# Second convolution of a graph network: the residual addition moved from VectorE to an identity product in TensorE and a copy by ScalarE

## The reference, cut to what matters

```python
h = x @ W;  dis = rsqrt(deg)
agg = segment_sum(h[src] * (dis[src] * dis[dst])[:, None], dst) + h * (dis * dis)[:, None]
return agg + b
# around both steps:
x = _layernorm(x + gcn_layer(relu(gcn_layer(x, W1, b1)), W2, b2), axis=-1)
```

## Time and profile before

| what | value |
|---|---|
| median of 3 runs | 10529.21 us (10516.9 to 10536.39) |
| the profiled execution | 10513.06 us |
| its span, first to last instruction | 10510.6 us |
| DVE busy over the span | 8002.5 us (76%) |
| POOL busy over the span | 7840.4 us (75%) |
| PE busy over the span | 6426.3 us (61%) |
| ACT busy over the span | 5904.7 us (56%) |

### The profile page before, as it was taken

How to read it: one execution, slowest core, us unless ns; L and a number is a source line. 1 busy time by engine, 2 the same in 40 slices (tenths; PEclk the granted TensorE clock), 3 DMA queues, 4 the chain that set the end, 5 groups by cost and what they waited for, 6 DMA issues and landing times. The chain is left out here.

```text
span 10510.6 us, 142293 instructions
## 1 busy us (share of the span) xinstructions
PE 6426.3 (61%) x32436; PEld 5258.3 (50%) x32436; DVE 8002.5 (76%) x33105; ACT 5904.7 (56%) x13869; POOL 7840.4 (75%) x7586
## 2 busy tenths in 40 slices
PE   6037666667774666667755666786457675654444
PEld 3026655555664666667755666674235443432222
DVE  8359899956667999999988888655558777874444
ACT  0026577767776999978957777432125443432222
POOL 7767688867776888766637777687777777878887
PEclk8569988878886555578868888665558765765555
DMA  3999888832223777634424555464336443432222
GB/s 114 330 299 314 286 289 289 289 123 75 76 74 121 234 236 235 207 126 139 142 87 160 173 175 177 145 172 120 92 104 183 143 116 99 139 111 65 63 65 60
DMA packets 1019500, 1694.47 MB, mean 161 GB/s; under 512 B 304877, under 2 KB 535080, under 8 KB 1018594
## 3 DMA queue, kind: packets, MB, share of 16 engines
q1 hardware_dynamic: 782752, 1361.06, 38.8%
q0 software_dynamic: 175936, 218.82, 9.3%
q10 hardware_dynamic: 59970, 105.49, 2.9%
HBM read 988.03 MB, written 707.78 MB: 161 GB/s over the span
## 5 line engine op out<-in xcount | busy, mean ns | idle before, releaser
L1351 POOL DMA_INDIRECT g_got<-scaled,row_src x2352 | 2230.1, 948 | 751.5 <-issue 631.8
L903 DVE SCALAR_TENSOR_TENSOR g_sums<-g_got,first,g_sums 128x128 f32<-128x128 f32 (+3 forms) x3136 | 871.6, 278 | 1159.5 <-DMA g_got<-scaled,row_src 1148.4
L299 PE MATMUL g_a_p_z<-sb_L_gnn_W,g_a_u_t 128*128 128x128 f32 (+3 forms) x2574 | 603.8, 373 | 592.5 <-DVE g_sums L1073 197.4
L1186 ACT COPY g_a_u_t<-g_a_p_t 128x512 f32<-128x512 f32 (+3 forms) x495 | 224.8, 454 | 1222.2 <-PE g_a_p_t L1138 637.3
L907 DVE SCALAR_TENSOR_TENSOR g_sums<-g_sums,cont,g_got 128x128 f32<-128x128 f32 (+3 forms) x3128 | 881.3, 282 | 0.0
L299 PEld LDWEIGHTS g_a_p_z<-sb_L_gnn_W,g_a_u_t 128*128 128x128 f32 (+1 forms) x2574 | 443.1, 245 | 759.9 <-ACT g_a_u_t L1186 398.3
L299 PE MATMUL g_bb_p_z<-sb_L_gnn_W,g_bb_u_t 128*128 128x128 f32 (+2 forms) x4302 | 755.8, 336 | 84.7 <-DVE g_bb_z L1078 77.0
L299 PEld LDWEIGHTS g_bb_p_z<-sb_L_gnn_W,g_bb_u_t 128*128 128x128 f32 x4302 | 676.0, 237 | 135.6 <-issue 108.9
L1186 ACT COPY g_bb_u_t<-g_bb_p_t 128x1024 f32<-128x1024 f32 (+2 forms) x294 | 233.6, 795 | 774.6 <-PE g_bb_p_t L290 774.1
L2475 POOL DMA_INDIRECT gb_got<-x,row_src x392 | 404.8, 1033 | 242.1 <-POOLq L178 138.1
L458 POOL DMA_INDIRECT f_got<-in_x,idx_dst x396 | 463.2, 1170 | 139.8 <-issue 120.1
(11 more groups left out here) (496 smaller groups left out, 23955.6 us busy)
## 6 DMA issues: line engine op xcount, KB each, us to landing
raw<-gb_u SPq DMA_DIRECT2D x98, 768.0 KB, 3.9
xs<-f_o ACTq DMA_DIRECT2D x97, 516.0 KB
f_x<-in_x ACTq DMA_DIRECT2D x97, 512.0 KB
g_bb_own<-in_x SPq DMA_DIRECT2D x97, 512.0 KB
wide<-g_bb_o SPq DMA_DIRECT2D x97, 512.0 KB
g_bb_own<-wide SPq DMA_DIRECT2D x97, 512.0 KB
g_bb_res<-in_x SPq DMA_DIRECT2D x97, 512.0 KB
x<-g_bb_o SPq DMA_DIRECT2D x97, 512.0 KB
```

The costliest lines, as they stand in the source:

```text
L299: last = nc.tensor.matmul(dst_psum[0:p, q * g * width:(q * g + n) * width], turned_tile[0:n * k, q * P:q * P + p], weight[0:n * k, 0:n * w ...
L903: nc.vector.scalar_tensor_tensor(out=self.firsts, in0=new, scalar=first[:, col], in1=self.firsts, op0=ALU.mult, op1=ALU.add).then_inc(run_ ...
L1186: last = nc.scalar.copy(to, source)
L1351: pool.indirect_dma_start(got[b.s4][:, c * row:(c + 1) * row], None, table, bass.IndirectOffsetOnAxis(ap=index[:, b.n * CH + c:b.n * CH + ...
```

## The change

It holds for the `b` node of this pass alone (`joins`: it has a residual, no last weight and no edges). The product's stage on PE now also waits for `gained`, and behind each of the 8 products by the weight it adds a product of the identity matrix with the residual's 128 columns onto the same place of the bank. DVE's `rows` of b is gone from its list. A new ACT stage `take_rows` (lag 1) waits for `multiplied` and copies the bank's 1024 columns to `g_bb_z`, raising `rows_ready`; it stands between `evacuate` of a and `normalise` of a.

```diff
+                self.joins = self.normal and not self.deep and edges is None
...
-                times_weight(self.p_z, self.u_t[b.s], self.weight, p, j, self.k, self.m).then_inc(m.multiplied, 1)
+                if self.joins:
+                    nc.tensor.wait_ge(m.gained, b.n + 1)
+                    for q in range(j):
+                        to = self.p_z[0:p, q * D:(q + 1) * D]
+                        nc.tensor.matmul(to, self.u_t[b.s][:, q * P:q * P + p], self.weight[:, :], start=True, stop=False)
+                        last = nc.tensor.matmul(to, ident[0:p, 0:p], self.res_s[b.s][0:p, q * D:(q + 1) * D], start=False,
+                                                stop=True)
+                    last.then_inc(m.multiplied, 1)
+                else:
+                    times_weight(self.p_z, self.u_t[b.s], self.weight, p, j, self.k, self.m).then_inc(m.multiplied, 1)
+
+            def take_rows(self, b):
+
+                p, j = self.r.pj(b)
+                m = self.m_
+                nc.scalar.wait_ge(m.multiplied, b.n + 1)
+                if b.after(len(self.z_s)):
+                    nc.scalar.wait_ge(m.finished, b.n + 1 - len(self.z_s))
+                nc.scalar.copy(self.z_s[b.n % len(self.z_s)][0:p, 0:j * D], self.p_z[0:p, 0:j * D]).then_inc(m.rows_ready, 1)
...
-                    return self.on(lag, every, (self.factors, 3), (self.rows, 1), (self.variance, 1))
+                    return self.on(lag, every, (self.factors, 3), (self.variance, 1))
...
-                    return self.on(lag, every, (self.root, 2), (self.evacuate, 0)), self.on(lag, every, (self.normalise, 3))
+                    return (self.on(lag, every, (self.root, 2), (self.evacuate, 0)),
+                            self.on(lag, every, (self.take_rows, 1), (self.normalise, 3)))
...
-                            factors, rows, variance = others_of
-                            stages += [*in_a((na.combine, 0), (na.factors, 3)), factors, *in_a((na.rows, 1)), rows,
+                            factors, variance = others_of
+                            stages += [*in_a((na.combine, 0), (na.factors, 3)), factors, *in_a((na.rows, 1)),
...
-                            stages = in_a((na.root, 2)) + ahead + in_a((na.evacuate, 0), (na.normalise, 3)) + behind
+                            stages = in_a((na.root, 2)) + ahead + in_a((na.evacuate, 0)) + behind[:1] + in_a((na.normalise, 3)) + behind[1:]
```

## The result

The changed kernel takes 10897.12 us in the median of 4 runs (10892.56 to 10933.97), the kernel before 10525.06 (4 runs, 10516.9 to 10536.39): 1.036 times as long, 95% interval 1.0336 to 1.0385. The prediction was 10887 us, in a range of 10700 to 11060. The execution that was profiled is the longest of the four: 10933.97 us, span 10932.2.

A forecast was written before the change was run, and what follows sets the result against it. DVE was taken to bound the pass at 9.10 us a turn; the new loop's terms sum to 25.91 us for two turns, 3.85 more a turn over 93 turns, 358 us, giving 10887 us, range 10700 to 11060.

The forecast's parts named there:

- The step that decides: Wait for `gained` moves from DVE's addition to PE's product, where PE must stand still until 6.4 us later.
- The loop's way through SP's store: Normalisation, SP's store, residual load, POOL's bias, PE's product, ACT's copy, normalisation two blocks on: 25.91 us for two turns.
- The terms: Times of the steps from normalisation through store, load, bias, product, transposes, evacuations and copy, summed to 25.91 us.
- 93 x 3.85 = 358 us: Loss over the pass: 12.95 us a turn against 9.10, counted for 93 of 98 turns.
- Unequal pairs of stores: Expected in the changed profile: stores of `b` blocks 12 to 14 us apart on average, perhaps in unequal pairs.
- Taken from DVE: DVE's addition, 1.13 us of its sequence a turn; at best 0.67 won, and worth nothing behind the loop.
- POOL's floor: POOL's own work of 8.43 us a turn, limiting any gain to 0.67 us a turn, 65 us over 97 turns.
- The residual is never late for PE: Rival: PE's wait lengthens no loop and the pass falls to POOL's 8.43 us a turn, 10464 us; chance 0.07.
- Only the bank tile counts: Rival: PE and ACT on the one `g_bb_p_z` set the turn, 9.02 to 9.9 us, around 10550 us; chance 0.10.
- PE stays at the half clock: Rival: all 32 records and the transposes at half clock add 1.9 us a turn, 11064 us; chance 0.08.
- DVE's 62%: DVE's busy share in the pass, forecast to fall from 98% to about 62%.
- POOL's 65%: POOL's busy share in the pass, forecast to fall to about 65%.

The follow-up runs named there:

- e2: Kernel before, with PE's product of a `b` block also waiting for the biased residual it does not read, no work added: 10798 us, 1.0257 of before.
- e3: Changed kernel without PE's wait for `gained`; the identity multiplies the bias row, and POOL's bias frees the residual buffer: 10491 us, 0.9967 of before.
- e1: Changed kernel with the residual loads of `a` and `b` blocks one turn earlier, into four buffers instead of two: 10493 us, 0.9965 of before.
- e7: Changed kernel with the `b` residual first, not last, among a turn's loads in SP's list: 10857 us, 1.0316 of the kernel before.
- e11: Changed kernel run once more, unedited, for a second trace: 10902 us (one run), 12.73 us a turn.
- e5: The kernel of e1 with the transposes of `b` ahead of its product in PE's list: 10740 us, 1.0208 of the kernel before.
- e9: Changed kernel with the identity product in two pieces of 512 columns instead of eight of 128, opening each bank: 10906 us, 1.0355 of before.

## Why the prediction was right

The place of the loss, its mechanism and its size came out as argued.

*The step that decides*, the wait for `gained` moved to PE, is shown by e2 (wait alone: slower by 266 us), e3 (all the work, no wait: faster) and e1 (wait kept, residual earlier: faster). The loop's way through SP's store is shown by e1 and, in sign, by e7; that the buffers were not what held the loads back is read from SP's waits, since e1 changed both at once.

*The terms* as measured in the loop above, against the predicted: store to load 3.03 (2.87 + 0.03); issue to bias 7.25 (7.03); bias to product 2.49 (2.35); product 6.28 (5.35); transposes to evacuation 1.08 (1.05); evacuations 0.91 and 0.47 (1.01 and 0.48); copy 0.91 (1.01); normalisations 1.55 and 3.20 (1.56 and 3.17). The sum is 27.17 against 25.91, three quarters of the difference being the product: I had put half of its 32 records at the low pace, and in the timeline 24 of them ran at it (0.63 us a pair, the last six records 0.39 a pair), at a granted clock of 0.56 in the mean. The alternating pattern's ring goes through such a slow product too, since its other product, which does not wait, lies beside the ring. What shortens it is above all the landing. Followed ring by ring through the timelines (45 rings of e11, 61 of the even part of the first profile), it took 6.5 us from issue to bias in the mean against 7.4, and the product 5.9 against 6.1; two turns took 25.9 against 27.2 us. Why the load lands sooner there stays open.

*The turns.* 93 x 3.85 = 358 us were predicted for the pass; store to store the first profile has 397 more than before, e11 359 (1235.0 against 875.9). The median of the runs lies 5 us from e11's execution. Part of the closeness (10 us) is luck. In e11's mean the product was half a microsecond longer than the 5.35 I had taken, and the landing half a microsecond shorter than the 7.03, so that two errors cancel in the sum of 25.91; in the even pattern of the first profile both were longer than predicted. Unequal pairs of stores had been named as possible, but not that they would be the shorter pattern; and PE, which was to wait in nearly every turn, does so in the first profile (80 times) but only in every second turn of e11.

*Taken from DVE:* worth nothing behind the loop, as predicted, and worth 39 us (10531.9 to 10492.7) once the loop is opened, of at most 65 that POOL's floor allowed.

*The rivals.* "The residual is never late for PE" would have given 10464; that is what e1 brought about, at 10493. "Only the bank tile counts" is excluded by e1: with the bank tile's loop unchanged the turn falls to POOL's 8.47. "PE stays at the half clock" was half true: of e11's products two that had waited ran at 0.55 (above) and 0.71, and one that had not at 1.00.

```profile
1825.88:1830.92 5.04, 5.04 (x32) 5.02 (x32) 0.00 (x0) 0.00 (x0) 0.71 0.64 241
```

*The shares.* DVE's 62% came out as 60%. POOL's 65% was 54%: I had divided its 8.43 us, which hold the gaps of about 0.3 us between gathers, where the profile counts busy time alone.

## What to carry to other kernels

When an operand moves to another engine, ask when that engine's place in its list comes, and not only whether the operand is ready where it is used today: here it was ready 0.65 us before DVE needed it and 6.4 us after PE would. In lists that wait in order, follow what stands behind the new wait until it reaches the transfer that fills the operand; if it does, the sum round the ring, divided by the number of turns it spans, is the new time of a turn, as long as no engine has more work than that (in e1 POOL's 8.4 us is what remains). Such a ring is opened by starting the transfer one turn earlier (buffers and a lag, e1), and it can be closed again through the next load by a small reordering (e5).

## What the runs showed of the hardware

In these products the records took time by their moving columns: 4 records of 512 columns and 16 of 128 lasted 3.54 us at the granted clock 1.00 (e9), and 32 records of 128 columns, the same 4096 columns in all, 3.62 (e11). Twelve weight loads fewer gave no more than that difference. And the clock made the change self-worsening: with the new waits the granted clock of the pass fell from 0.87 to 0.75 (0.79 in e11), and the product that the ring goes through lasted 5.04 and 6.39 us in two turns of e11, where one that had not waited lasted 3.62. The same work without the long waits ran at 0.96 to 0.97 (e3, e1).
